# All attention products in strips of 32 weight columns, with the causal mask in constant stack rows and four small triangles

## What is computed

```
H, dk = 16, 8
q = rope(q, positions); k = rope(k, positions)
scores = einsum('bhqd,bhkd->bhqk', q, k) / sqrt(dk)
scores = where(causal, scores, -inf)
attn = softmax(scores, axis=-1)
out = einsum('bhqk,bhkd->bhqd', attn, v)
return einsum('bsd,ed->bse', out, W_o)
```

## Time and profile before

| | |
|---|---|
| median of 3 runs | 1900.53 us (1895.67 to 1906.98) |
| profiled execution, its own time | 1904.92 us |
| its span | 1903.1 us |
| mean granted TensorE clock | 0.895 |
| PE / PEld busy | 1553.2 / 709.6 us |
| DVE / ACT / POOL busy | 1338.6 / 1011.8 / 1006.9 us |
| PE instructions (matmuls) | 7115 |
| attention lead | about 1160 to 1225 us |
| first maxima | 1225 to 1265 us |
| the eight turns | 1265 to 1652 us |

### The profile page before, as it was taken

The page is one execution under the profiler, slowest core; times in us unless marked ns, Lnnn a source line. Parts: engine busy times, 40 slices in busy tenths (PEclk is TensorE's granted clock), DMA queues, the critical chain, the costliest instruction groups (busy, mean ns, idle before and its releaser), DMA issues. The chain is left out here.

```text
span 1903.1 us, 22232 instructions
## 1 busy us (share of the span) xinstructions
PE 1553.2 (82%) x7115; PEld 709.6 (37%) x7115; DVE 1338.6 (70%) x1497; ACT 1011.8 (53%) x1647; POOL 1006.9 (53%) x534
## 2 busy tenths in 40 slices
PE   6788787788878877786791876788899999899998
PEld 4222222222222222221271664544555555474443
DVE  6699999998999999999662112566667776257545
ACT  5867676766666777774230432434555555446220
POOL 1599999998999999999624243201111110025000
PEclk9889888988988889987775897869999999989999
DMA  4463433243434333434003222503332221101546
GB/s 153 102 156 101 112 101 89 79 105 84 112 101 112 100 83 86 109 90 102 28 32 106 51 71 60 152 17 86 86 86 77 74 74 37 51 1 37 123 102 142
DMA packets 101777, 164.94 MB, mean 87 GB/s; under 512 B 16678, under 2 KB 55374, under 8 KB 99990
## 3 DMA queue, kind: packets, MB, share of 16 engines
q1 hardware_dynamic: 93510, 159.07, 32.7%
q0 software_dynamic: 2688, 4.80, 0.8%
q10 hardware_dynamic: 5504, 0.09, 0.2%
HBM read 106.32 MB, written 26.04 MB: 70 GB/s over the span
## 5 line engine op out<-in xcount | busy, mean ns | idle before, releaser
L481 POOL TENSOR_TENSOR PR<-H,CS 128x1024 f32<-128x1024 f32 x256 | 598.6, 2358 | 69.7 <-DVE H L457 31.4
L457 DVE TENSOR_TENSOR_SCAN H<-DA,X 128x1024 f32<-128x1024 f32 x192 | 431.2, 2273 | 0.0
L348 PE MATMUL psY<-PR,fold 128*64 128x512 f32 x1024 | 291.5, 663 | 4.5 <-POOL PR L481 4.5
L445 DVE TENSOR_TENSOR X<-DU,psB 128x1024 f32<-128x1024 f32 x192 | 235.8, 1228 | 71.8 <-PE psB L328 45.8
L433 ACT ACTIVATE DA<-DT,negA 128x511 f32<-128x511 f32 x384 | 250.6, 710 | 1.1
L1475 ACT ACTIVATE a_PT<-a_psS 128x512 f32<-128x512 f32 x320 | 181.1, 601 | 117.0 <-PE a_psS L1379 112.9
L1522 DVE TENSOR_REDUCE a_MX<-a_psM 128x1 f32<-128x384 f32 (+3 forms) x352 | 203.6, 635 | 23.6 <-PE a_psM L1394 22.2
L492 POOL TENSOR_TENSOR XS<-DU,BS 128x1024 f32<-128x1024 f32 x64 | 150.9, 2358 | 0.0
L298 PE MATMUL pp<-work,convW 128*128 (+1 forms) x256 | 145.8, 701 | 5.3 <-ACT pre L386 5.3
L1393 PE MATMUL a_psM<-a_kst,a_qst 72*128 72x512 bf16 (+3 forms) x512 | 139.0, 317 | 13.4 <-DVE a_MX L1522 10.9
L457 DVE TENSOR_TENSOR_SCAN H<-X,XS 128x1024 f32<-128x1024 f32 x64 | 146.1, 2283 | 0.5 <-POOL XS L492 0.4
(11 more groups left out here) (295 smaller groups left out, 2634.6 us busy)
## 6 DMA issues: line engine op xcount, KB each, us to landing
CS<-c_rows SPq DMA_DIRECT2D x128, 256.0 KB, 3.9
DT<-W SPq DMA_DIRECT2D x64, 256.0 KB, 4.3
DU<-ab SPq DMA_DIRECT2D x64, 256.0 KB, 4.2
BS<-c_rows SPq DMA_DIRECT2D x64, 256.0 KB, 4.3
g_CB<-c_tok SPq DMA_DIRECT2D x32, 512.0 KB, 10.9
scratch_q<-a_partsq SPq DMA_DIRECT2D x24, 384.0 KB, 3.3
a_qst<-scratch_q SPq DMA_DIRECT2D x8, 1152.0 KB
a_kst<-scratch_k SPq DMA_DIRECT2D x24, 384.0 KB
```

Of the source, the lines that this page charges most:

```text
L348: last = nc.tensor.matmul(psY[h * HP:(h + 1) * HP, n % 2 * T:(n % 2 + 1) * T], fold[:, :], chunk(PR[n % 4], h), start=False, stop=n >= NS - 2)
L445: nc.vector.tensor_tensor(both(X[s % 2][:, :]), DU[p][:, at:at + 2, :], psB[:, :].unsqueeze(1).to_broadcast([P, 2, T]), ALU.mult).then_inc ...
L457: nc.vector.tensor_tensor_scan(H[s % 4][:, :], decay, x, 0.0, ALU.mult, ALU.add).then_inc(scan_done, 1)
L481: nc.gpsimd.tensor_tensor(both(PR[s % 4][:, :]), both(H[s % 4][:, :]), CS[q % 2][:, s // 2 % 2, :].unsqueeze(1).to_broadcast([P, 2, T]), A ...
```

## The change

`strips` issues a product as four matmuls of 32 weight columns, each to its own 32 output partitions; all products of the turns go through it, with the same moving operand. The transposes G and F become products with the identity as the moving operand, in fp32. The transposes of the maxima become three of 32 columns (4 query blocks x 24 rows as 96 rows) in place of four of 24.

The mask is split. Sixteen constant rows are put between the parts and the maxima in both stacks (`SPANS = 16` spans of 32 positions, `MROW` = 88): in `kst` a row of the identity for each span of keys, in `qst` the row of -1e30 where the query's span is before it. These mask whole later spans of 32 within the product. What is left are four triangles of 32 x 32 on the diagonal (`mask_strips`). The constants are made by three small DVE operations and put into the four stacks by four DMAs in the lead. The maxima go through the scratch as 96 rows of 128 elements.

```diff
     ident = W[:, 0:P]
-    MROW = 72
+    PROW = 72
+    SPANS = T // 32
+    MROW = PROW + SPANS
     KR = MROW + 3
...
         NMB = sb("NMB", [P, QT, 3, HEADS // 2], BF16)
-        MTS = [sb(f"MTS{i}", [24, T], BF16) for i in range(2)]
+        MTS = [sb(f"MTS{i}", [24 * QT, P], BF16) for i in range(2)]
         psM = [ps(f"psM{i}") for i in range(3)]
...
         ones_ready, ones_loaded = sem("ones_ready"), sem("ones_loaded")
-        ones3 = sb("ones3", [3, T], BF16)
+        kconst, qconst = sb("kconst", [SPANS + 3, T], BF16), sb("qconst", [SPANS, T], BF16)
         st_loaded = [sem("st_loaded0"), sem("st_loaded1")]
...
+        def strips(out, lhsT, rhs, start=True, stop=True):
+            for c in range(0, P, 32):
+                last = nc.tensor.matmul(out[c:c + 32, :], lhsT[:, c:c + 32], rhs, start=start, stop=stop)
+            return last
+        def mask_strips(out, mask):
+            for c in range(0, P, 32):
+                last = nc.tensor.matmul(out[c:c + 32, c:c + 32], identb[:, c:c + 32], mask[:, c:c + 32], start=False, stop=True)
+            return last
         def pe_use(pe, name, n, t2, p1):
...
             if name[0] in "qk":
-                last = nc.tensor.matmul(mb[:, :], w("w" + name), hT[:, ds(t2 * T, T)], start=True, stop=True)
+                last = strips(mb[:, :], w("w" + name), hT[:, ds(t2 * T, T)])
             elif name == "V":
                 for i in range(QT):
-                    last = nc.tensor.matmul(mb[:, i * P:(i + 1) * P], HB[:, i * P:(i + 1) * P], w("wv"), start=True, stop=True)
+                    last = strips(mb[:, i * P:(i + 1) * P], HB[:, i * P:(i + 1) * P], w("wv"))
             elif name[0] == "G":
                 for j in range(QT):
-                    last = nc.tensor.transpose(mb[:, j * P:(j + 1) * P], OT[int(name[1]) % 2][:, j * P:(j + 1) * P], ident)
+                    last = strips(mb[:, j * P:(j + 1) * P], OT[int(name[1]) % 2][:, j * P:(j + 1) * P], ident)
             elif name[0] == "M":
-                rows = mb[:, 0:T // 2].bitcast(BF16)
-                for j in range(QT):
-                    last = nc.tensor.transpose(rows[0:24, j * P:(j + 1) * P], NMB[:, j, :, :].rearrange("p s h -> p (s h)"), identb[:, :])
+                rows, maxima = mb[:, 0:P // 2].bitcast(BF16), NMB[:, :, :, :].rearrange("p j s h -> p (j s h)")
+                for c in range(3):
+                    last = nc.tensor.transpose(rows[32 * c:32 * c + 32, :], maxima[:, 32 * c:32 * c + 32], identb[:, :])
             elif name == "F":
                 for j in range(QT):
-                    last = nc.tensor.transpose(mb[:, j * P:(j + 1) * P], OTK[:, j, :], ident)
+                    last = strips(mb[:, j * P:(j + 1) * P], OTK[:, j, :], ident)
             else:
-                last = nc.tensor.matmul(mb[:, :], w("wo"), OF[:, :], start=True, stop=True)
+                last = strips(mb[:, :], w("wo"), OF[:, :])
             last.then_inc(mb_ready, 1)
...
         def pe_scores(pe, t, p, k, u):
...
                 out = psS[S_BUF[5 * k + u]][:, col:col + wide]
-                nc.tensor.matmul(out, kst[p][:, at + i * P:at + (i + 1) * P], qst[p][:, at + i * P:at + T], start=True, stop=False)
-                last = nc.tensor.matmul(out[:, 0:P], identb[:, :], mkq[:, :], start=False, stop=True)
+                strips(out, kst[p][:, at + i * P:at + (i + 1) * P], qst[p][:, at + i * P:at + T], stop=False)
+                last = mask_strips(out[:, 0:P], mkq)
             last.then_inc(S_ready, 1)
...
         def pe_maxima(pe, n0, p, half, a, b):
...
                     out = psM[M_BUF[half * NG + a + g]][:, x * wide:(x + 1) * wide]
-                    nc.tensor.matmul(out, qst[p][0:72, at + j * P:at + (j + 1) * P], kst[p][0:72, at:at + wide], start=True, stop=False)
-                    last = nc.tensor.matmul(out[:, j * P:wide], identb[:, :], mqk[:, :], start=False, stop=True)
+                    strips(out, qst[p][0:MROW, at + j * P:at + (j + 1) * P], kst[p][0:MROW, at:at + wide], stop=False)
+                    last = mask_strips(out[:, j * P:wide], mqk)
                 last.then_inc(M_ready, 1)
...
         def pe_values(pe, t, p, g, i):
...
                 half = "AB".index(name[1])
-                rows = mb[:, 0:T // 2].bitcast(BF16)
+                rows = mb[:, 0:P // 2].bitcast(BF16)
                 if not isinstance(t, int) or t >= 0:
                     dve.wait_ge(m_loaded[half], 16 * t + 16)
-                v.tensor_copy(MTS[half][:, :], rows[0:24, :]).then_inc(mb_used, 1)
+                v.tensor_copy(MTS[half][:, :], rows[0:24 * QT, :]).then_inc(mb_used, 1)
             elif name == "F":
...
         def load_stack(sp, b, pb):
             sp.wait_ge(parts_stored, 64 * b + 64)
-            sp.dma_start(qst[pb][0:MROW, :], scratch_q[pb].rearrange("a c (j h) t -> (a c j) (h t)", h=HEADS)).then_inc(st_loaded[pb], 16)
+            sp.dma_start(qst[pb][0:PROW, :], scratch_q[pb].rearrange("a c (j h) t -> (a c j) (h t)", h=HEADS)).then_inc(st_loaded[pb], 16)
             for a in range(3):
...
         def send_maxima(sp, b, half, used, pb):
             sp.wait_ge(mb_used, used)
-            rows = m_scratch[ds(48 * b + 24 * half, 24), :]
+            rows = m_scratch[ds(48 * b + 24 * half, 24), :].rearrange("r (x q) -> (r x) q", q=P)
             sp.dma_start(rows, MTS[half][:, :]).then_inc(m_stored[half], 16)
             sp.wait_ge(m_stored[half], 16 * b + 16)
-            sp.dma_start(qst[pb][MROW:MROW + 3, half * 8 * T:(half + 1) * 8 * T],
-                           rows.rearrange("(s h) t -> s (h t)", s=3)).then_inc(m_loaded[half], 16)
+            sp.dma_start(qst[pb][MROW:MROW + 3, half * 8 * T:(half + 1) * 8 * T].rearrange("s (h j q) -> s h j q", h=8, j=QT),
+                           rows.rearrange("(j s h) q -> s h j q", j=QT, s=3)).then_inc(m_loaded[half], 16)
...
             def _(sp):
...
                     sp.dma_start(gtok[:, 4 * b:4 * b + 4, :], y_tok[1 + b * T:1 + b * T + T, :].rearrange("(k p) d -> p k d", p=P)).then_inc(y_loaded[b], 16)
-                sp.wait_ge(ones_ready, 1)
+                sp.wait_ge(ones_ready, 3)
                 for i in range(2):
-                    sp.dma_start(kst[i][MROW:KR, :].rearrange("s (h t) -> s h t", h=HEADS),
-                                 ones3[:, :].unsqueeze(1).to_broadcast([3, HEADS, T])).then_inc(ones_loaded, 16)
+                    sp.dma_start(kst[i][PROW:KR, :].rearrange("s (h t) -> s h t", h=HEADS),
+                                 kconst[:, :].unsqueeze(1).to_broadcast([SPANS + 3, HEADS, T])).then_inc(ones_loaded, 16)
+                    sp.dma_start(qst[i][PROW:MROW, :].rearrange("s (h t) -> s h t", h=HEADS),
+                                 qconst[:, :].unsqueeze(1).to_broadcast([SPANS, HEADS, T])).then_inc(ones_loaded, 16)
                 store_parts(sp, 0, 0)
...
                 pe.wait_ge(st_loaded[0], LOADS)
+                pe.wait_ge(ones_loaded, 64)
                 pe_maxima(pe, 0, 0, 0, 0, NG)
...
                 pe.wait_ge(m_loaded[0], 16)
-                pe.wait_ge(ones_loaded, 32)
                 pe.wait_ge(h_ready, B)
...
             def _(dve):
-                nc.vector.memset(ones3[:, :], 1.0).then_inc(ones_ready, 1)
+                nc.vector.memset(kconst[:, :], 1.0).then_inc(ones_ready, 1)
+                nc.vector.tensor_copy(qconst[:, :].rearrange("s (g x) -> s g x", x=32),
+                                      w("mask_kq")[0:SPANS, 0:SPANS].unsqueeze(2).to_broadcast([SPANS, SPANS, 32])).then_inc(ones_ready, 1)
+                dve.wait_ge(ones_ready, 1)
+                nc.vector.tensor_copy(kconst[0:SPANS, :].rearrange("s (g x) -> s g x", x=32),
+                                      ident[0:SPANS, 0:SPANS].unsqueeze(2).to_broadcast([SPANS, SPANS, 32])).then_inc(ones_ready, 1)
                 dve_residual(dve, 0)
```

## The result

The changed kernel takes 1917.48 us (median of 8 runs, 1911.94 to 1920.98); the kernel before, run beside it, 1898.1 us. The ratio is 1.009, 95% interval 1.0067 to 1.0113: about 17 us slower, where 19.5 us faster was predicted. The time lies inside the stated range of 1866 to 1930 us, but in the part that belonged to a rival. The profiled execution spans 1916.8 us, against 1903.1 before.

A forecast was written before the change was run, and what follows sets the result against it. PE was taken as the fullest engine, though not alone. Its terms, 18.0 + 28.2 + 1.0 - 16.8, make 30.4 us less; two thirds (20.3), with +1.8 and -1, give -19.5: from 1900.5 to 1881 us, range 1866 to 1930.

The forecast's parts named there:

- Term 2, the blocks: Score and maxima blocks on PE: mean 0.17 us instead of 0.1975, over 1024 blocks -28.2 us, bounds -31 and +84.
- Term 1, the changes: Changes between strips and full width around value products on PE: 0.20 us in and out, 90 pairs go, -18.0 us.
- Term 3, G and F: The transposes G and F as fp32 products on PE: 0.88 us for 0.46, 40 times 0.42, +16.8 us.
- the two thirds that are passed on: In the turns, two thirds of PE's saving of 30.4 us shortens them, 20.3 us; a third becomes longer waits for DVE and ACT.
- Term 4, the constants at "nothing": Small things; the constants' 1.1 MB in the lead cost nothing behind idle DMA engines, 6 us if that cover were gone.
- The row of DVE's copy: DVE's copy of the transposed maxima: 0.2 us less each, 3.2 us less on DVE, -1 us on the path.
- issue bounds PE: Rival (0.31): in score and maxima blocks, handing PE 8 pairs a block limits it; 1927 us at 0.027 a pair, up to 1984.
- point of decision: For blocks on PE, the issue limit decides from 0.025 us to a pair of load and matmul, a mean block of 0.199.
- the likeliest case: As forecast (0.5): PE's saving in the turns shortens the kernel to 1881 us, own range 1868 to 1891.
- The rule of the Trainium skill: About 60 cycles of overhead per matmul on PE: a block of 8 pairs takes at least 0.20 us, giving +15 us.
- The clock: Sign in the turns: the forecast is wrong if the granted clock leaves 0.99.

The follow-up runs named there:

- e2: The changed kernel with the stack loads from the third sequence on cut to one head of sixteen: 1889.2 us, ratio 0.9926 to the kernel before.
- e3: The kernel before with the same cut of the stack loads to one head of sixteen: 1893.3 us, ratio 0.9956 to the uncut kernel before.
- e13: The changed kernel with the constant rows of the k stacks sent as 16 and 3 rows apart: 1908.4 us, ratio 1.0044 to the kernel before.
- e8: The kernel before with the changed kernel's constant transfers added and waited for at the same place: 1910.0 us, ratio 1.0037 to the kernel before.

## Why the prediction was wrong

The direction was wrong. Three things explain it. In the profiled executions, from the first exp to the end of the last turn, the strips give 7.9 us with small stack loads, where 20.3 was forecast for the turns; the stack loads cost the changed kernel 15.0 us more than the one before, where nothing was forecast; and the first exp comes 6.6 us late. 15.0 + 6.6 - 7.9 = 13.7 us, by which the attention ended later, against the forecast -19.5. The ratios, which rest on more executions, put 23 us (uncertain by some 8) on the stack loads (e2 and e3) and 9 (by some 5) on the constants (e13; 7 by e8); for the 17 us measured this leaves 15 to the strips, which is a remainder and no measurement. The two accounts agree in sign, in size only within these uncertainties.

- **Term 2, the blocks, right.** Forecast 0.14 and 0.19 for two widths, measured 0.14 and 0.19.
- **Term 1, the changes, right in size.** Ahead of a value product 0.15, of which 0.06 was the triangle, became 0.03, which is the small triangles alone: 0.09. 0.57 of the product of 256 columns became 0.44: 0.13. That is 0.22 for the pair where 0.20 was taken.
- **Term 3, G and F, right on PE, short on the path.** A G takes as long as forecast, 0.87 us for 0.88; the rows:

```profile
1314.91 1.08 PE L1351 MATMUL a_mb<-W,a_OT 128*32 128x128 f32 x32
1315.78 0.43 PE L1351 MATMUL a_psS<-a_qst,a_kst 91*32 91x512 bf16 x4
```

  Undone, PE does 9 us less (3.5 in three turns), where 16.8 less 40 pairs of changes at 0.2 makes 8.8. In these three turns nearly all of it reached the end (3.3 of 3.5 us); two thirds was too low here.
- **PE's work in all, right; the two thirds that are passed on, wrong.** Forecast 30.4 us less, measured 28.5 over the turns, 4.4 in a turn at full clock. Of it 7.9 us reached the end even with small loads, 0.28 instead of two thirds; in the three turns at full clock it was 6.5 of 13.2, half. That is 12.4 us of the forecast. What took the rest is only in part known: PE's idle time grew by 20.6 us, of which seven short stops behind instruction packets are 7.5, and in the fifth and sixth turn the clock was low for a while.
- **Term 4, the constants at "nothing", wrong.** They cost 5 to 9 us. The cover that I named was the idle DMA engines (0.13 busy), and the price without cover was 1.1 MB at the rate of all engines, 6 us. The transfer did not run on all engines: it went by one, for 14 us each time, and what stood behind it in SyncE's queue was the first store, 6.5 us late. I counted bytes and forgot the shape and the queue. The row of DVE's copy was right (0.2 taken):

```profile
L1578 DVE COPY a_MTS<-a_mb 96x128 bf16<-96x128 bf16 x16 | 3.5, 216 | 3.2 <-PE a_mb L1375 3.2
```

- **The rival "issue bounds PE", right in its direction, wrong in its mechanism and place.** It gave 1914 to 1927, and 1917 was measured. But a pair takes 0.018 us (0.142 for 8 in a block of 256 columns), below its point of decision of 0.025, and the stretches in which PE has its instructions are as fast as the likeliest case said. The forecast's own sentence held the true cause, that instruction loads would come three times as often (26 became 79), and used it only to raise a chance. This is the largest of the steps that failed: it got no price, neither for what an instruction load waits for nor for what else is on the DMA engines at that time, 2.3 MB of stack at a share of 0.8 in a turn. It cost 15 us by the traces, 23 by the ratios. That the time fell between this rival's 1914 and 1927 is luck. The rule of the Trainium skill (TensorEngine Tiling, Performance Considerations, Instruction Overhead) would have come out at 1914, close by accident; by its 0.20 us a block, the block of 0.14 would not exist.
- **The clock.** "The forecast is wrong if the granted clock leaves 0.99" came true: 0.95 in the turns, 0.50 for 4.5 us behind a stop. It follows the stops; with small loads three turns ran at 1.00, and two later ones fell to 0.50 for a while. What the low clock cost by itself was not measured.

What stays open: how much of the short stops of 0.9 to 2.0 us could be avoided, since some remained in every version with strips; why instruction packets came through two of the six stack loads without a long stop and not through the other four; and what took most of PE's saving in the turns. A version in which the instruction loads always pass the stack loads was not found.

## What to carry to other kernels

When a change multiplies the instructions of an engine in unrolled code, price their loading as a transfer: count the loads, and ask which bulk transfer they will stand behind, since a stop for one that was late among 2.3 MB took up to 4.7 us, with a low clock after it. Use the finer form where it pays (score and maxima blocks, next to the value products), and not for the transposes G and F, where it costs both time and instructions. For every new transfer look at its outer size and at what stands behind it in its queue; 16 and 3 rows instead of 19 were worth 5 to 9 us. And where a profile puts a wait down to "issue", look at what the program waits for at that place before blaming the instructions.

## What the runs showed of the hardware

- PE's instructions come in packets of 16 KB in queue q8, 0.9 to 1.5 us each, one to 256 loads and matmuls (20232 to 79 packets from 1265 to 1652 us). PE goes on 1.3 to 1.6 us after a late packet has ended. Among the bulk of a stack load packets can be 9.4 to 13.3 us apart instead of some 4, and PE then stands for up to 4.7 us; with small stack loads no such stop is left in the turns. The Trainium skill (Runtime: NRT & Kernel Launch, Instruction fetch mechanics) says that the cost of crossing such a block is "mostly hidden". The kernel before agrees (no wait for issue over 0.8 us with 26 loads), the changed one with 79 loads does not.
- Strips of 32 weight columns can follow each other at 0.018 us to a pair of load and matmul: eight pairs in 0.142 us, in the maxima blocks of 256 columns at 1410.88 and 1411.02.
- A transfer of 19 rows of 16 KB takes 13.9 us on one engine; split into 16 and 3 rows, it and the 16-row transfer behind it are issued in 3.4 and 5.3 us (e13).
